# First attention: the products of probabilities and values issued at the end of a step

## The chip, the cores and the metric

The program runs on one core of one Trainium2 chip. The metric is the device time of one execution in microseconds; the median of several runs is compared. Five engines run their own instruction lists and meet through semaphores: TensorE (PE, matrix products and, through them, transposes), VectorE (DVE), ScalarE (ACT), GpSimd (POOL) and SyncE (SP, which only issues DMAs here).

## The reference, cut to what matters

The program computes two layers, each an attention and a mixture of experts, on a residual stream x of 8 batches, 256 tokens and 128 features:

```
x = x + L0_attn(layernorm(x)); x = x + L0_ffn(layernorm(x))
x = x + L1_attn(layernorm(x)); x = x + L1_ffn(layernorm(x))
```

The change lies in the first attention, L0_attn. It has 16 query heads and 4 key heads of 8 features, rotary positions and a causal softmax:

```
q = rope((x @ Wqa @ Wqb).reshape(b, s, 16, 8)); k, v likewise from Wkva, Wkvb, repeated for 4 query heads each
scores = einsum('bqhd,bkhd->bhqk', q, k) * scale          # causal mask, softmax over k -> w
out = einsum('bhqk,bkhd->bqhd', w, v).reshape(b, s, 128) @ Wout + bout
```

L0_ffn follows: a gate chooses two of 8 experts for each token, and the tokens are sorted by expert into 39 tiles. In the kernel this routing is done beside the attention, group by group of batches, and the expert phase begins when the first groups are placed.

## The kernel before, in words

The first attention is a software pipeline over the 8 batches. A **step** is a pair (c, s): c runs from -2 to 10, s over 0, 1, 2, 3, and u = 4c + s numbers it. Each engine has the same loop over the steps (`for c, s in STEPS0`) in its own block, with its own work in each. Within a step TensorE works on several batches at once, in an order that is written out by hand. In the kernel before it is this:

- scores: for batch c, the score products from which the row maxima come (`max_scores`, L1934, three banks), and interleaved with them, for the batch-and-group number p = u - 5, the scores that go to the softmax (`prob_scores0`, L1944 and L1946, three banks). p counts 4 groups for each of 8 batches;
- masks: `masks0` (L1919, L1921) adds the causal mask to the three banks of maxima, so that VectorE may reduce them (`maxima`, L917);
- at s = 0, `turn_max` (L1955) for batch c - 1;
- weighing: `weigh0(u - 6)` (L1970, L1973), 16 products of values and probabilities of group p = u - 6, into bank BO;
- at s = 0, `give_out0(c - 3)` (L2035), the output projection;
- at s = 1, `spread0(c + 1)` (L1982 to L1988), which spreads the rotated queries and keys over the array's rows, in three banks, and `turn_x0(c + 2)` (L1996), the transposes of the normalised input, in one bank;
- at s = 2, `turn_o(c - 2)` (L2018) and `project0(c + 2)` (L2004, L2005, L2009; three banks);
- at s = 3, `turn_back(c - 2)` (L2027);
- where a routing step is due, `route_rows`: `turn_rows` (L1855), `gate_rows` (L1869) or the ranks (`older_rows` and `rank_rows`, L1878 to L1895). For the groups of batches from number 2 on, `gate_rows` is instead issued directly behind the masks.

**The ring of banks.** PSUM has eight banks. Bank BO belongs to the weighing alone; all other products take the next of the seven others in the order of `ring0()` (NRING = 7), and `take` makes TensorE wait until the product that had the bank seven places earlier has been read. `weigh0` takes no bank of the ring. In step (c, 1) the order is three banks of maxima, three of probabilities, three of `spread0`, one of `turn_x0`; in step (c, 2) three, three, one for `turn_o`, three of `project0`.

**What waits for the weighing.** ScalarE's copy of its result, `copy_o0` (L1574): the second half of batch c - 2 in the steps with s = 1, the first half of batch c - 1 in those with s = 3. In a step with s = 1 ScalarE's list is: the exponentials of that step (`exps0`, L1568), `key_copy` (L1548), `copy_o0`, `stack0` (L1554, two copies of the second and third bank of `spread0`). `exps0(p)` waits for the weighing of p - 2. GpSimd masks the probabilities (`mask_probs`, L683) behind the exponentials, and the weighing of p waits for that.

VectorE's list in a step begins with routing (`take_logits`, `choose`, `give_slots`) where it is due, then, by s: `turn` (L898) at s = 3; `residual0` (L951) and `moments_of` at s = 1; `maxima` in every step; `add_max` (L934) and `norm` at s = 0; `normalise` (L941, L944) and `norm_rows` (L1001) later. GpSimd has `mask_probs`, the roots (L668), the sum and difference of the rotation (L692, L698) and the scattering of the rows to the experts' buffer (L738). Behind the last step VectorE stages the first experts' weights (L1117), and TensorE turns the first gathered tile (L2081) once batch 7 has its residual.

Of the kernel before, what the change touches and what calls it, by code (L numbers as in the profile page):

```python
# [18 lines left out]
B, S, D = 8, 256, 128  # L19
# [141 lines left out]
def build(nc, inp, out, last_stage=3):  # L161
    ctx = ExitStack()
    with ctx:
# [204 lines left out]
        def wait(eng, name, b, k):  # L368

            sm, c, before = tables[-1][name]  # L370
            value = b * c + k
            if isinstance(value, int) and value <= 0:
                return
            eng.wait_ge(sm, value + before + 1)

        def signal(ins, name):
            ins.then_inc(tables[-1][name][0], 1)
# [24 lines left out]
        def inside(b):  # L402
            return 0 <= b < B
# [7 lines left out]
        def due(l, u, work):  # L411

            for u0, q in FROM[l].items():
                if u - u0 == AFTER[l][q][work]:
                    return q
            return -1
# [21 lines left out]
        def gates_first(l, q):  # L438
            return q >= COUNTED
# [125 lines left out]
        def _(sp):  # L565
            sp.dma_start(X[:, 0:FIRST, :], inp["x"][0:FIRST].rearrange("t p d -> p t d")).then_inc(x_loaded[0], 16)
            sp.dma_start(misc[:], inp["c_misc"][:, :]).then_inc(ident_loaded, 16)
            for sm in [a for a, _, _ in s0.values()]:
                sp.sem_inc(sm, 1)
# [1250 lines left out]
        def _(pe):  # L1820
# [9 lines left out]
            def take(kind, b, k=0):  # L1830

                assert next(taken) == (kind, b, k)
                at = AT0[kind, b, k] - NRING
                if at >= 0:
                    if RING0[at][0] in ROUTING:
                        for sm, value in routing_read(0, *RING0[at]):
                            pe.wait_ge(sm, value)
                    else:
                        wait(pe, *read_of(*RING0[at]))
                return bank0(kind, b, k)  # L1840
# [6 lines left out]
            def turn_rows(l, q, take):  # L1847

                m = ms[l]
                t0, t1 = TILES[q]  # L1850
                pe.wait_ge(m["normed"], t1 + 1)
                for n in range(rT_banks(q)):
                    bank = take("rT", q, n)
                    for t in range(t0 + 4 * n, min(t0 + 4 * n + 4, t1)):
                        mm = pe.transpose(bank[:, (t - t0 - 4 * n) * P:(t - t0 - 4 * n + 1) * P], rsc[:, t % SLOTS, 0, 0:D], ident)  # L1855
                    mm.then_inc(m["rT"], 1)

            def gate_rows(l, q, take):

                m = ms[l]  # L1860
                if q == 0:
                    pe.wait_ge(w_loaded[l], 16 * (6 if l == 0 else 4))
                pe.wait_ge(m["rT_copied"], sum(rT_banks(a) for a in range(q + 1)) + 1)
                w = D + E if l == 0 else E
                per = 2 if l == 0 else size(q)
                for n in range(gate_banks(l, q)):
                    bank = take("gate", q, n)
                    for t in range(per):
                        mm = pe.matmul(bank[:, t * w:(t + 1) * w], rowsT[:, (per * n + t) * P:(per * n + t + 1) * P], gates[l][:], start=True, stop=True)  # L1869
                    mm.then_inc(m["gated"], 1)  # L1870

            def older_rows(l, q, bank, count):

                t0, t1 = TILES[q]
                h = t1 - t0
                if (l, q) == (0, 0):
                    pe.wait_ge(moe_cast, 3)
                pe.matmul(bank[:, 0:h * E], identb[:], regionb[:].unsqueeze(1).broadcast_to((P, h, E)), start=True, stop=False)  # L1878
                for t in range(t0):
                    pe.matmul(bank[:, 0:h * E], onesb[:], picked[:, t, :].unsqueeze(1).broadcast_to((P, h, E)), start=False, stop=False)  # L1880
                    if count is not None:
                        pe.matmul(count[:, 0:E], onesb[:], picked[:, t, :], start=(t == 0), stop=False)

            def rank_rows(l, q, bank, count):

                m = ms[l]
                t0, t1 = TILES[q]
                h = t1 - t0
                pe.wait_ge(m["picked"], q + 1 + 1)
                for t in range(t0, t1 - 1):  # L1890
                    pe.matmul(bank[:, (t + 1 - t0) * E:h * E], onesb[:], picked[:, t, :].unsqueeze(1).broadcast_to((P, t1 - 1 - t, E)), start=False, stop=False)
                pe.matmul(bank[:, 0:h * E], beforeb[:], picked[:, t0:t1, :].rearrange("p t e -> p (t e)"), start=False, stop=True).then_inc(m["ranked"], 1)
                if count is not None:
                    for t in range(t0, t1):
                        mm = pe.matmul(count[:, 0:E], onesb[:], picked[:, t, :], start=False, stop=(t == t1 - 1))  # L1895
                    mm.then_inc(m["counted"], 1)

            def route_rows(l, u, take):

                q = due(l, u, "turn")  # L1900
                if q >= 0:
                    turn_rows(l, q, take)
                q = due(l, u, "gate")
                if q >= 0 and not gates_first(l, q):
                    gate_rows(l, q, take)
                q = due(l, u, "rank")
                if q >= 0:
                    bank = take("rank", q)
                    count = take("count", q) if q == COUNTED else None
                    older_rows(l, q, bank, count)  # L1910
                    rank_rows(l, q, bank, count)
# [46 lines left out]
            def weigh0(p):  # L1958

                b, g = p // 4, p % 4  # L1960
                half, own = g // 2, g % 2
                wait(pe, "masked", 0, p + 1)
                if g == 0:
                    wait(pe, "v_copied", b, 1)
                    wait(pe, "o_copied", b, 0)
                if g == 2:
                    wait(pe, "o_copied", b, 1)
                values = [vst0[b % 4][:, 4 * t + 2 * half:4 * t + 2 * half + 2, :].rearrange("p a c -> p (a c)")[:, 32 * own:32 * own + 32] for t in range(2)]
                for j in range(4):
                    pe.matmul(ps[32 * j:32 * j + 32, BO, half * S:(half + 1) * S], values[0], probs[p % 2][:, j * S:(j + 1) * S],  # L1970
                              start=(own == 0), stop=False)
                for j in range(4):
                    mm = pe.matmul(ps[32 * j:32 * j + 32, BO, half * S + P:(half + 1) * S], values[1], probs[p % 2][:, 4 * S + j * P:4 * S + (j + 1) * P],  # L1973
                                   start=False, stop=(own == 1))
                signal(mm, "pv")
# [62 lines left out]
            for c, s in STEPS0:  # L2038
                u = 4 * c + s
                if (c, s) == (-2, 2):  # L2040
                    pe.wait_ge(w_copied, 2)
                if (c, s) == (-1, 1):
                    pe.wait_ge(consts_cast, 6)
                    pe.wait_ge(loaded, 16 * 2)
                for part in range(4):
                    if inside(c):
                        max_scores(c, s, part)
                    if 0 <= u - 5 < 4 * B and part < 3:
                        prob_scores0(u - 5, part)
                if inside(c):  # L2050
                    masks0(c, s)
                if due(0, u, "gate") >= COUNTED:
                    gate_rows(0, due(0, u, "gate"), take)
                if s == 0 and inside(c - 1):
                    turn_max(c - 1)
                if 0 <= u - 6 < 4 * B:
                    weigh0(u - 6)
                if s == 0 and inside(c - 3):
                    give_out0(c - 3)
                if (c, s) == (-1, 1):  # L2060
                    turn_x0(1)
                if s == 1 and inside(c + 1):
                    spread0(c + 1)
                if s == 1 and inside(c + 2) and c != -1:
                    turn_x0(c + 2)
                if s == 2 and inside(c - 2):
                    turn_o(c - 2)
                if s == 2 and inside(c + 2):
                    project0(c + 2)
                if s == 3 and inside(c - 2):  # L2070
                    turn_back(c - 2)
                route_rows(0, u, take)
            assert next(taken, None) is None
            wait(pe, "residual", B - 1, 1)
            pe.wait_ge(ms[0]["shared"], sum(gate_banks(0, q) for q in range(LATE)) + 1)
# [265 lines left out]
```

## Time and profile before

| | us |
|---|---|
| median of 3 runs | 568.91 (568.16 to 569.52) |
| span of the profiled execution | 568.9 |
| TensorE busy in it | 482.2 (85%) |
| VectorE busy | 359.5 (63%) |
| ScalarE busy | 296.2 (52%) |
| GpSimd busy | 290.9 (51%) |
| granted TensorE clock, mean | 0.904 of full speed |

The span of the profiled execution and the median of the runs differ by less than 0.1 us. In the rows below, times are microseconds from the start of the span. A row of a timeline gives the start, the duration, the engine, the line of the kernel, the operation, its output and input, their shapes and how many instructions are merged; in brackets stands how long the engine was idle just before, and what ended that. Matrix products are pipelined: the recorded end of one lies behind the start of the next, so that distances are read from start to start. The steps with weighing run from about 47 us (u = 6, which is c = 1, s = 2) to 187 us (u = 37). The spread of step (c, 1) starts at 62.07 for c = 2, at 79.17 for c = 3, at 96.25 for c = 4, at 115.42 for c = 5 and at 135.01 for c = 6; for c = 7 there is none.

### The profile page before, as it was taken

What the parts mean: (1) busy time and instruction counts of PE and PEld (TensorE: products, weight loads), DVE (VectorE), ACT (ScalarE), POOL (GpSimd) and SP (SyncE); (2) the same over time, 40 slices, a digit from 0 to 9 for tenths busy, and PEclk for the clock granted to TensorE, in tenths of its full rate; (3) what the DMA queues carried; (4) which work ended last, traced back from release to release, by engine and by line L of the source; (5) the groups of instructions that cost most, each with busy time, mean ns of one, the idle gap of its engine ahead of it and who ended that gap; (6) DMA issues with size and microseconds to landing.
All of it is one profiled execution on the core that took longest, in us unless ns stands there. A gap on an engine that the chain in (4) does not pass through costs nothing. (4 is left out here: it accounts for less than half of the span.)

```text
span 568.9 us, 14158 instructions
## 1 busy us (share of the span) xinstructions
PE 482.2 (85%) x4435; PEld 384.5 (68%) x4435; DVE 359.5 (63%) x1190; ACT 296.2 (52%) x832; POOL 290.9 (51%) x381
## 2 busy tenths in 40 slices
PE   5779999999998499999667889999899747999980
PEld 3556666656555399999636667677677527899980
DVE  3685677877863535463597788897785863533323
ACT  2224555445553176667536687666753515567650
POOL 3624445448476454565642445443763874356550
PEclk9987999989975589999978899999898977999995
DMA  6999200000000131232199900300000013123217
GB/s 215 323 312 364 88 1 2 1 1 30 13 24 30 43 83 40 81 88 71 34 356 318 318 25 1 150 2 3 20 21 11 30 40 77 55 70 98 72 39 226
DMA packets 28375, 53.71 MB, mean 94 GB/s; under 512 B 4816, under 2 KB 24208, under 8 KB 27248
## 3 DMA queue, kind: packets, MB, share of 16 engines
q1 hardware_dynamic: 23216, 42.17, 23.5%
q0 software_dynamic: 4544, 9.45, 5.0%
q10 hardware_dynamic: 544, 1.20, 0.6%
q8 instruction: 38, 0.62, 0.5%
q14 instruction: 33, 0.27, 0.1%
HBM read 42.32 MB, written 29.81 MB: 127 GB/s over the span
## 5 line engine op out<-in xcount | busy, mean ns | idle before, releaser
L1654 ACT ACTIVATE probs<-ps,w1s 128x128 f32<-128x128 f32 x312 | 89.3, 370 | 47.1 <-PE ps L2090 47.1
L797 POOL DMA_INDIRECT ybuf<-yt,xg x78 | 76.2, 978 | 59.1 <-DVE yt L1183 50.8
L2090 PE MATMUL ps<-xgT,w1s 128*128 128x128 f32 x624 | 86.5, 283 | 1.6 <-ACT xgT L1645 0.9
L738 POOL DMA_INDIRECT xbuf<-rsc,sloti x64 | 63.1, 986 | 40.6 <-DVE sloti L1054 14.8
L2098 PE MATMUL ps<-w,probs 128*128 x624 | 82.2, 276 | 0.0
L2090 PEld LDWEIGHTS ps<-xgT,w1s 128*128 128x128 f32 x624 | 79.1, 199 | 3.4 <-ACT xgT L1645 1.8
L917 DVE TENSOR_REDUCE negm<-ps 128x2 f32<-128x512 f32 (+1 forms) x96 | 60.3, 685 | 27.9 <-PE ps L1921 21.3
L2098 PEld LDWEIGHTS ps<-w,probs 128*128 128x128 f32 x624 | 75.6, 192 | 0.0
L1568 ACT ACTIVATE probs<-ps 128x512 f32<-128x512 f32 x96 | 51.2, 603 | 35.6 <-PE ps L1944 35.1
L1117 DVE COPY w1s<-w 128x516 f32 x78 | 33.9, 434 | 44.0 <-issue 40.2
L683 POOL TENSOR_SCALAR_AFFINE_SELECT probs<-probs 128x512 f32<-128x512 f32 x64 | 39.2, 637 | 40.6 <-ACT probs L1568 40.0
L832 POOL TENSOR_SCALAR_AFFINE_SELECT probs<-probs 128x512 f32<-128x512 f32 x64 | 39.4, 642 | 37.7 <-ACT probs L1757 37.5
L1183 DVE TENSOR_TENSOR yt<-ps,bias 128x128 f32<-128x128 f32 x78 | 22.7, 291 | 46.1 <-PE ps L2098 44.9
L1757 ACT ACTIVATE probs<-ps 128x512 f32<-128x512 f32 x64 | 34.8, 601 | 11.9 <-PE ps L2150 11.9
L1437 DVE SCALAR_TENSOR_TENSOR X<-ps,GT,X 128x128 f32<-128x128 f32 x80 | 27.9, 349 | 7.1 <-PE ps L2190 5.1
L1645 ACT ACTIVATE xgT<-ps 128x128 f32<-128x128 f32 x78 | 22.8, 293 | 18.3 <-PE ps L2081 18.2
L2081 PE MATMUL ps<-misc,xg 128*128 128x128 f32 x78 | 22.2, 287 | 11.4 <-DMA xg<-xbuf 6.9
L2174 PE MATMUL ps<-probs,vst 128*32 128x128 f32 x512 | 22.7, 284 | 8.9 <-POOL probs L832 6.7
L1970 PE MATMUL ps<-probs,vst 128*32 128x256 f32 x256 | 23.5, 444 | 3.4 <-POOL probs L683 3.4
L668 POOL TENSOR_TENSOR rstd<-var,halves 128x4 f32<-128x4 f32 (+2 forms) x17 | 16.9, 996 | 18.4 <-issue 15.3
L1944 PE MATMUL ps<-qst,keys 32*128 32x512 f32 x48 | 21.5, 504 | 5.1 <-DVE qst L934 2.5
L692 POOL TENSOR_TENSOR rot<-rot 128x512 f32<-128x512 f32 x8 | 10.2, 1279 | 28.3 <-DVE rot L898 28.3
(276 smaller groups left out, 1057.6 us busy)
## 6 DMA issues: line engine op xcount, KB each, us to landing
xbuf<-in_c_pads SPq DMA_DIRECT2D x16, 1122.0 KB, 18.8
xg<-xbuf SPq DMA_DIRECT2D x78, 66.0 KB, 1.9
w<-in_w SPq DMA_DIRECT2D x2, 2064.0 KB, 24.0
w<-in_w SPq DMA_DIRECT2D x2, 2048.0 KB, 35.9
w<-ybuf SPq DMA_DIRECT2D x5, 512.0 KB, 5.9
ybuf<-yt,xg POOLq DMA_INDIRECT x78, 2.3
probs<-in_c_sel ACTq DMA_DIRECT2D x2, 512.0 KB, 5.2
bias<-in_b SPq DMA_DIRECT2D x2, 512.0 KB, 31.1
```

What stands on the lines that cost most here:

```text
L683: last = pool.affine_select(out=diag, in_=diag, compare_op=ALU.is_ge, fill=0.0, base=0, pattern=[[0, 4], [1, P]], channel_multiplier=-1)
L738: pool.indirect_dma_start(out=xbuf[l][:, :], out_offset=bass.IndirectOffsetOnAxis(ap=sloti[:, k, t:t + 1], axis=0), in_=rsc[:, t % SLOTS, ...
L797: pool.indirect_dma_start(out=ybuf[l][:, :], out_offset=bass.IndirectOffsetOnAxis(ap=xg[n % AHEAD][:, D:D + 1].bitcast(I32), axis=0), in_= ...
L832: signal(pool.affine_select(out=chunk, in_=chunk, compare_op=ALU.is_ge, fill=0.0, base=0, pattern=[[0, 4], [1, P]], channel_multiplier=-1) ...
L917: signal(dve.tensor_reduce(dst, src, AX.X, ALU.max, negate=True), "maxed")
L1117: dve.tensor_copy(w1s[n % STAGED][:], w1[:, ds(of_tile[n] * W1, W1)]).then_inc(ms[l]["staged"], 1)
L1437: signal(dve.scalar_tensor_tensor(tile, bank1("look", b, look)[:, n * D:(n + 1) * D], GT[:, 2 * b + t, NC - 1 - at - n:NC - at - n], tile, ...
L1568: signal(act.activation(probs[p % 2][:, 512 * n:512 * (n + 1)], bank0("prob", p // 4, 3 * (p % 4) + n), ACT.Exp, scale=QK_SCALE), "probs_d ...
L1654: ins = act.activation(hidT[n % 3][:, c * P:(c + 1) * P], ps[:, q, c * P:(c + 1) * P], ACT.Gelu if l == 0 else ACT.Relu, bias=w[:, FF + c: ...
L1757: signal(act.activation(probs[u % 2][:, n * 4 * P:(n + 1) * 4 * P], bank1("prob", u // 4, 2 * (u % 4) + n), ACT.Copy), "probs_done")
L2090: mm = pe.matmul(ps[:, n % 2, c * P:(c + 1) * P], w[:, c * P:(c + 1) * P], xgT[n % 2][:], start=True, stop=True)
L2098: mm = pe.matmul(ps[:, 6 + n % 2, 0:D], hidT[n % 3][:, c * P:(c + 1) * P], w2[:, ds(e * FF + c * D, D)], start=(c == 0), stop=(c == FC - 1))
```

## The change

`weigh0(u - 6)` is taken from its place behind the masks and `turn_max` and put at the end of the step, behind `route_rows`. Nothing else is changed: the same instructions with the same waits, the same ring of banks, the same lists of the other engines.

```diff
                 if s == 0 and inside(c - 1):
                     turn_max(c - 1)
-                if 0 <= u - 6 < 4 * B:
-                    weigh0(u - 6)
                 if s == 0 and inside(c - 3):
                     give_out0(c - 3)
...
                 if s == 3 and inside(c - 2):
                     turn_back(c - 2)
                 route_rows(0, u, take)
+                if 0 <= u - 6 < 4 * B:
+                    weigh0(u - 6)
```

## Rows read from the trace of the kernel before

**Rows 1.** Windows: busy time by engine, granted clock, DMA share, GB/s, 48 to 190 us and 54 to 104 us

```profile
48.00:190.00 142.00, 131.87 (x1200) 85.26 (x1192) 96.84 (x258) 68.78 (x147) 81.04 (x118) 0.88 0.12 47
54.00:104.00 50.00, 47.84 (x464) 32.27 (x459) 37.91 (x83) 25.89 (x57) 24.76 (x36) 1.00 0.13 51
```

**Rows 2.** Waits of TensorE, 40 to 190 us: total, times, longest

```profile
PE ps L1970 <- POOL probs L683: 3.4, 1, 3.4
```

**Rows 3.** Timeline of TensorE, steps (3, 1), (3, 2) and into (3, 3)

```profile
78.38 0.64 PE L1970 MATMUL ps<-probs,vst 128*32 128x256 f32 x8
...
79.17 0.39 PE L1982 MATMUL ps<-hi,selr 128*128 128x256 f32 x1
...
80.46 0.38 PE L1996 MATMUL ps<-misc,xn 128*128 128x128 f32 x2
80.77 0.39 PE L1934 MATMUL ps<-keys,qst 32*128 32x256 f32 x3
...
81.58 0.46 PE L1946 MATMUL ps<-qst_late,keys 32*128 32x512 f32 x1
81.97 0.50 PE L1921 MATMUL ps<-aboveb,identb 128*128 128x256 bf16 x3
...
83.19 0.66 PE L2018 MATMUL ps<-misc,o 128*128 128x128 f32 x4
83.68 0.60 PE L2004 MATMUL ps<-xnT,wq 128*128 128x256 f32 x2
```

**Rows 4.** Timeline of VectorE and ScalarE, the same steps

```profile
78.34 1.89 DVE L917 TENSOR_REDUCE negm<-ps 128x4 f32<-128x512 f32 x3 [0.20 <-PE ps L1921]
...
80.08 0.38 ACT L1574 ACTIVATE o<-ps 128x256 f32<-128x256 f32 x1
...
80.35 1.09 ACT L1554 ACTIVATE qst<-ps 128x512 fp32r<-128x512 f32 x2
...
82.36 1.89 DVE L917 TENSOR_REDUCE negm<-ps 128x2 f32<-128x512 f32 x3 [2.13 <-PE ps L1921]
```

**Rows 5.** Timeline, step (3, 3): ScalarE's copy behind the weighing

```profile
88.22 0.44 PE L2027 MATMUL ps<-misc,on 128*128 128x128 f32 x2
...
88.35 0.38 ACT L1574 ACTIVATE o<-ps 128x256 f32<-128x256 f32 x1 [0.26 <-PE ps L1973]
```

**Rows 6.** Timeline of VectorE and TensorE, steps (4, 1) and (4, 2)

```profile
95.75 1.89 DVE L917 TENSOR_REDUCE negm<-ps 128x4 f32<-128x512 f32 x3
...
98.12 0.39 PE L1934 MATMUL ps<-keys,qst 32*128 32x256 f32 x3
...
99.05 0.22 PEld L1921 LDWEIGHTS ps<-aboveb,identb 128*128 128x128 bf16 x3 [0.24 <-issue]
```

**Rows 7.** Timeline, step (5, 3)

```profile
122.35 0.22 DVE L1047 TENSOR_TENSOR ranks<-first,ps 128x64 f32<-128x64 f32 x1 [1.12 <-PE ps L1892]
...
123.83 0.46 PE L1944 MATMUL ps<-qst,keys 32*128 32x512 f32 x1 [1.20 <-DVE rot L898]
...
125.82 1.08 PE L1970 MATMUL ps<-probs,vst 128*32 128x256 f32 x8
```

**Rows 8.** Timeline, end of step (6, 3) and step (7, 1)

```profile
142.90 0.63 PE L1855 MATMUL ps<-misc,rsc 128*128 128x128 f32 x4 [0.49 <-DVE negm L917]
...
149.47 0.42 DVE L951 TENSOR_TENSOR X<-X,ps 128x256 f32<-128x256 f32 x1
```

**Rows 9.** Timeline, steps (8, 3) to (9, 1)

```profile
175.74 1.08 PE L1970 MATMUL ps<-probs,vst 128*32 128x256 f32 x8
...
177.26 0.19 DVE L1038 TENSOR_TENSOR picked<-first 128x32 bf16<-128x32 f32 x1
...
177.66 0.23 PE L1878 MATMUL ps<-regionb,identb 128*128 128x32 bf16 x1
...
178.46 0.22 DVE L1047 TENSOR_TENSOR ranks<-first,ps 128x64 f32<-128x64 f32 x1 [1.01 <-PE ps L1892]
...
186.06 1.08 PE L1970 MATMUL ps<-probs,vst 128*32 128x256 f32 x8 [3.39 <-POOL probs L683]
```

## The prediction, written before the changed kernel was run

> **What bounds the kernel now.** First the windows: in the 142 us that hold the weighing TensorE is busy for 131.87, and no other engine reaches 97 [rows 1]. So the stage goes at TensorE's pace, and what counts is each stretch in which it stands still. Next its waits: the only wait of a weighing for its masks is one of 3.4 us [rows 2]. That one, at 186.06, is at u = 37, where the order of the step has nothing to move [rows 9]. So no weighing in its present place waits for anything that a later place could hide. Then the timeline, which shows what the weighing itself hides. It takes 0.79 us from start to start (78.38 to 79.17) [rows 3], and it takes no bank of the ring. While it runs, VectorE reduces the three banks of maxima that the masks have just closed (1.89 us in all) [rows 4]. The next products of the step take just those banks: in (c, 1) the second and third bank of the spread and the bank of `turn_x0` lie seven places behind the three maxima; in (c, 2) the three of `project0` do. That is read from the ring's order, not from a row.
>
> **The change part by part.** Nothing is added or removed: 32 weighings of 16 products keep their waits, and no DMA moves with them. GpSimd's and SP's lists are untouched. I reckon each batch from the start of its masks in (c, 2) against where they start now. A hand-over from one engine to the next I take as 0.14 us: TensorE's third probability product starts at 81.58, ScalarE's second `stack0` ends at 80.35 + 1.09 = 81.44 [rows 3, 4].
>
> *Term A, the spread held back.* In (3, 1) the masks end at 78.38 [rows 3]; VectorE's three reductions end at 78.34 + 1.89 = 80.23, 0.63 apart [rows 4]. `turn_x0` now starts at 80.46, with nothing to wait for. Moved up by the weighing's 0.79 it would start at 79.67, but its bank is free at 80.23 + 0.14 = 80.37. With its own 0.31 (80.46 to 80.77) and then the weighing's 0.79 the step ends at 81.47, against 80.77: 0.70 lost. Of the 0.79 only 0.09 finds work to do. For c = 2 and c = 5 I take the same. For c = 4 VectorE starts its reductions only at 95.75 and ends at 97.64 [rows 6]: 97.64 + 0.14 + 0.31 + 0.79 = 98.88 against 98.12, 0.76 lost. For c = 6 there is no `turn_x0`, and the last bank waits for the second reduction: about 0.41.
>
> *Term B, the copies behind the weighing.* In (c, 1) ScalarE's `copy_o0` waits for this step's weighing, and `stack0`'s two copies stand behind it in ScalarE's list. The second and third probability product of (c, 2) take the banks that these two copies read. Now the weighing is over at 79.17, long before `copy_o0` starts at 80.08. Afterwards it ends last of all, at 81.47. `copy_o0` starts 0.13 later (88.22 to 88.35 [rows 5]), `stack0` 0.27 after that (80.08 to 80.35) and ends 1.09 later: 82.96 [rows 4]. The third product starts at 83.10, the masks 0.39 later (81.58 to 81.97 [rows 3]) at 83.49. They now start at 81.97, so that A and B make 1.52, and B alone 0.82. For c = 2 and 5 I take 1.50. For c = 4: 98.88 + 2.02 = 100.90 against 99.05, 1.85 [rows 6]. For c = 6 the third product waits for the first of the two copies only: A and B about 1.00. B's bounds: 0, if ScalarE's copies overlap the products as now, and 1.1.
>
> *Term C, the projection.* With the weighing gone from between masks and `turn_o`, `project0` starts 0.43 + 0.49 = 0.92 after the masks' start (83.19 less 0.79 and 81.97; 83.19 to 83.68) [rows 3]. Its first bank is that of the first maxima: VectorE starts 0.39 after the masks (81.97 to 82.36), takes 0.63, and 0.14 to hand over: 1.16. So 0.24 for c = 2 and 3 each [rows 3, 4]. For c = 4, 5 and 6 the next step waits for VectorE's later work in any case, and C costs nothing.
>
> *Term D, (5, 3).* Ranks of the routing are due in (5, 2). VectorE is idle for 1.12 us until they come, then turns the rotation, and TensorE waits 1.20 us for that [rows 7]. The ranks now come ahead of the weighing, so VectorE starts 0.6 sooner against the masks, and the weighing covers part of the turn: I take a gain of 0.77. Its bounds are 0 and 1.20 plus what the clock adds. It stood at half, 1.2 GHz, behind that wait: the weighing at 125.82 shows 1.08 us for its first part where 0.64 is usual [rows 7, 3].
>
> *Term E, `turn_rows`* in (4, 3) and (6, 3). It takes the bank of the step's first maxima. At 142.90 it has waited 0.49 us for VectorE [rows 8], with the weighing already done. Afterwards the weighing comes behind that wait, not before it, and only part of its 0.79 falls where the next scores wait anyway. I take a loss of 0.39 and 0.48 (bounds 0 and 0.79 each).
>
> *Term F, (7, 1).* `gate_rows` comes 0.79 sooner, and so does `residual0` (149.47) [rows 8], whose bank the second probability product waits for: a gain of 0.35 (0 to 0.45).
>
> *Term G, the tail.* In (8, 3) the chosen experts are known at 177.26 + 0.19 = 177.45, but TensorE comes to the rank products at 177.66, because weighing and `turn_back` stand ahead, and VectorE goes on at 178.46 [rows 9]. The weighing out of the way, `turn_back` and the older ranks are done by 176.8, the rank products follow the choice at once, and VectorE goes on at about 177.85. The slots, eight scatters, and the last masks, for which the weighing at 186.06 waits, hang on this: a gain of 0.60 (0 to 0.8).
>
> In the steps (c, 0) `turn_max` stands ahead of the weighing before and after, `give_out0` (c from 3 on) moves up, and the next scores wait for `add_max` as now: nothing. In (1, 2), (1, 3) and (2, 0) the readers are early or the order is the same: nothing.
>
> *Sum.* c = 2: 1.50 + 0.24 = 1.74. c = 3: 1.52 + 0.24 = 1.76. c = 4: 1.85 + 0.39 = 2.24. c = 5: 1.50 - 0.77 = 0.73. c = 6: 1.00 + 0.48 = 1.48. c = 7: -0.35. Tail: -0.60. Together 7.0 us later. All behind the stage follows from its end, and keeps its length. The profiled span is 568.9, the median of the runs 568.91, so no correction is due: 568.9 + 7.0 = 575.9 us.
>
> The page "TensorE: Matmul & The Clock Gate" of the Trainium skill (its head table) calls ScalarE's queue strictly first in, first out. By that rule term B stands; if copies could pass one another, `stack0` would not wait for `copy_o0`, and the sum would be lower by B. No row of the kernel before shows a blocked ScalarE copy with ready ones behind it.
>
> **The rivals.**
>
> *Half of it.* Only the ring's wait for VectorE bites (A, C, E), and ScalarE's copies are hidden, say because they are handed over faster. For: `stack0`'s 1.09 us stand beside scores and masks of 1.6 us (80.77 to 82.40). Against: `copy_o0` cannot start before the weighing ends. Without B (0.8 for c = 2, 3 and 5, 1.1 for c = 4, 0.6 for c = 6: 4.1) 2.9 is left: 571.8 us.
>
> *The clock falls.* The new waits split TensorE's work in the steps (c, 1) and (c, 2) of five batches, some 1.7 us in each. Behind the 1.20 us wait of (5, 3) the granted clock was at half [rows 7]; part of a weighing there took 0.44 us more. A spell over a weighing and its neighbours I put at 1.0 to 1.6 us. Three or four spells and A to G: 580 to 582 us. Against it: from 54 to 104 us TensorE stood still for 2.2 us in all, and the clock stayed full [rows 1]. The same page, under "A second HAM failure mode: psum-queue depth-cycling", says that small idle gaps between groups of products, as they arise in cycling through PSUM banks, can make the clock swing between its levels; that would be this case.
>
> *Faster.* VectorE and ScalarE have the banks free in time, because TensorE's slack reaches back to them: the point is whether `turn_x0` can start within 0.1 us of the spread's last product. Then A, B, C and E are zero, D, F and G remain (1.7), and with the clock full in (5, 3) about 1.0 more: 568.9 - 2.7 = 566.2 us. Against: TensorE's products are in order, and the reductions cannot start before the masks.
>
> *Nothing.* TensorE's waits fall where it would have waited later: about 569. Against: the waits of (5, 3) and (4, 3) alone could take up such slack, and I have counted them.
>
> **How the numbers follow.** Forecast, 574 to 578: 0.55. Half of it, 571 to 574: 0.17. The clock, above 578: 0.18. No change: 0.03. Faster: 0.07. The likeliest is 575.9. The range 571.3 to 579.5 leaves out the faster cases and half of the clock's. A difference below 0.2% (1.1 us) is what the measurement can't tell from none. Faster by more 0.06, within it 0.04, slower by more 0.90.
>
> **What would show it.** In (3, 1) and its like the second bank of the spread starts about 0.35 us behind the first, with VectorE's reduction as its releaser, and `turn_x0` 0.14 behind the third reduction (A). ScalarE shows an idle stretch ahead of L1574 that ends with L1973, and TensorE one ahead of L1944 or L1946 that ends with L1554 (B). From (3, 2) to (4, 2) the masks stand 19.2 us apart (17.08 now, from 81.97 to 99.05, with 0.24 of C at c = 3 and 1.85 of A and B at c = 4). The 1.20 us wait of (5, 3) is gone or halved (D), and VectorE's ranks in (8, 3) come 0.4 us behind the choice (G). Wrong would be: no wait for L917 in the spread; a TensorE that stands at 1.2 GHz in stretches from 60 to 120 us; or a stage as long as before with a later stage changed.

## The result

The changed kernel took 578.8 us (median of 4 runs, 575.5 to 580.0). The recorded ratio to the kernel before is 1.0136 with a 95% interval of 1.0088 to 1.0184, which is 7.7 us (5.0 to 10.5) of 568.9; the plain medians, 578.8 and 568.91, lie 9.9 us apart, and a fourth execution of the kernel before, of 1082 us, is left out. In a second set, on another occasion, the changed kernel's median was 582.4 us (6 runs) and the ratio 1.0133 (1.0070 to 1.0197). So it is slower, clear of the noise, by less than 2%. The forecast was 575.9 us, slower. The profiled execution is 578.1 us long, 9.2 more than that of before. All ratios here leave out executions more than 1.5% above the fastest of their kernel.

The page of the changed kernel (busy time by engine, then the tenths of 40 slices):

```profile
span 578.1 us, 14158 instructions
PE 484.6 (84%) x4435; PEld 387.7 (67%) x4435; DVE 359.2 (62%) x1190; ACT 294.3 (51%) x832; POOL 290.3 (50%) x381
PE   4779889889898579999758889999899856999980
PEclk9787897998999579999969899996998976999995
```

The number of instructions is that of before and the busy times are nearly the same, so the 9.2 us are idle time and clock. TensorE's waits from 40 to 200 us (total, times, longest):

```profile
PE ps L1970 <- POOL probs L683: 4.3, 1, 4.3
PE ps L1944 <- ACT qst L1554: 1.9, 3, 0.6
PE ps L1987 <- DVE negm L917: 1.6, 4, 0.4
PE ps L1855 <- DVE negm L917: 1.5, 2, 0.9
PE ps L2004 <- DVE negm L917: 1.2, 4, 0.3
...
PE ps L1944 <- ACT qst_late L1554: 0.6, 1, 0.6
...
PE ps L1944 <- DVE rot L898: 0.4, 1, 0.4
PE ps L1946 <- ACT qst L1554: 0.4, 1, 0.4
```

The same list for the kernel before (40 to 190 us) has no wait for L1554 and none at L1987 or L2004, and it has these two:

```profile
PE ps L1944 <- DVE rot L898: 1.6, 2, 1.2
...
PE ps L1855 <- DVE negm L917: 0.5, 1, 0.5
```

So the waits for L1554 (the copies of term B; five of them, the last in (6, 2)) and those at L1987 (the spread, A) and L2004 (the projection, C; four each) are new. The wait at L1855 (E) has grown, and the one for L898 (D) is down. Steps (3, 1) and (3, 2), TensorE:

```profile
79.75 0.38 PE L1921 MATMUL ps<-aboveb,identb 128*128 128x256 bf16 x2
79.88 0.36 PE L1982 MATMUL ps<-hi,selr 128*128 128x256 f32 x1
...
80.76 0.39 PE L1987 MATMUL ps<-hi,selr 128*128 128x256 f32 x1 [0.40 <-DVE negm L917]
...
82.05 0.41 PE L1996 MATMUL ps<-misc,xn 128*128 128x128 f32 x2
82.39 0.64 PE L1970 MATMUL ps<-probs,vst 128*32 128x256 f32 x8
...
83.18 0.39 PE L1934 MATMUL ps<-keys,qst 32*128 32x256 f32 x3
...
84.33 0.46 PE L1944 MATMUL ps<-qst_late,keys 32*128 32x512 f32 x1 [0.65 <-ACT qst L1554]
...
85.22 0.50 PE L1921 MATMUL ps<-aboveb,identb 128*128 128x256 bf16 x3
85.56 0.60 PE L2018 MATMUL ps<-misc,o 128*128 128x128 f32 x4
86.45 0.75 PE L2004 MATMUL ps<-xnT,wq 128*128 128x256 f32 x2 [0.29 <-DVE negm L917]
```

and VectorE and ScalarE in them:

```profile
80.01 1.89 DVE L917 TENSOR_REDUCE negm<-ps 128x4 f32<-128x512 f32 x3 [0.20 <-PE ps L1921]
...
83.31 0.38 ACT L1574 ACTIVATE o<-ps 128x256 f32<-128x256 f32 x1 [2.34 <-PE ps L1973]
83.59 1.08 ACT L1554 ACTIVATE qst<-ps 128x512 fp32r<-128x512 f32 x2
```

They answer to [rows 3, 4]. The spread's second bank waits 0.40 us for the first reduction; `turn_x0` starts at 82.05, 0.15 behind the third (80.01 + 1.89 = 81.90). ScalarE stands idle for 2.34 us ahead of `copy_o0`, which starts 0.13 behind the weighing (83.18), and TensorE then waits 0.65 us for the first `stack0`. From the masks at 79.75 to those at 85.22 are 5.47 us; before, from the row below to 81.97 [rows 3], 3.90. That is 1.57 for A and B, where 1.52 was reckoned.

```profile
78.07 0.38 PE L1921 MATMUL ps<-aboveb,identb 128*128 128x256 bf16 x2
```

Some of the rest is the clock. In the windows the last number but two is the granted clock, as a share of full speed:

```profile
59.00:64.00 5.00, 5.00 (x39) 3.56 (x34) 2.02 (x4) 2.05 (x4) 1.92 (x3) 0.66 0.26 94
64.00:86.00 22.00, 19.64 (x186) 12.98 (x178) 13.10 (x27) 11.76 (x27) 8.75 (x14) 1.00 0.01 2
86.00:91.00 5.00, 4.71 (x30) 3.65 (x28) 3.51 (x7) 0.65 (x2) 1.56 (x3) 0.66 0.00 0
96.00:101.00 5.00, 4.97 (x40) 3.69 (x39) 4.80 (x15) 0.87 (x3) 2.05 (x3) 0.66 0.02 5
134.00:139.00 5.00, 4.98 (x41) 2.71 (x41) 2.63 (x6) 3.14 (x7) 3.95 (x5) 0.66 0.00 0
...
176.00:188.00 12.00, 9.62 (x106) 6.04 (x105) 5.68 (x26) 7.57 (x18) 10.40 (x17) 1.00 0.07 25
```

A mean of 0.66 over 5 us means that part of the window stood at half clock, 1.2 GHz. Between 59 and 101 us there are three such windows, where the execution of before had full clock from 54 to 104 us [rows 1]; in return the clock is full from 176 to 188 us, in the steps of c = 8, where before it stood at half (0.50). At the start of the experts (L2081) the two executions are 7.1 us apart (205.94 against 198.84); the other 2.1 us arise later, with unchanged code. How much of this belongs to the change and how much to the execution, one profile cannot tell.

### The profile page after: what moved, and what is told of

It reads as the page before. It is cut to its first block and busy times, and to the rows that moved or that the text cites. A ratio compares the mean times of both kernels' runs of the same rounds, so it can differ in the third digit from the quotient of the medians.

```text
span 578.1 us, 14158 instructions
## 1 busy us (share of the span) xinstructions
PE 484.6 (84%) x4435; PEld 387.7 (67%) x4435; DVE 359.2 (62%) x1190; ACT 294.3 (51%) x832; POOL 290.3 (50%) x381
## 5 line engine op out<-in xcount | busy, mean ns | idle before, releaser
L2081 PE MATMUL ps<-misc,xg 128*128 128x128 f32 x78 | 22.1, 287 | 11.8 <-DMA xg<-xbuf 6.9
L1970 PE MATMUL ps<-probs,vst 128*32 128x256 f32 x256 | 22.2, 422 | 4.3 <-POOL probs L683 4.3
L2150 PEld LDWEIGHTS ps<-qst,kst 32*128 32x128 f32 x256 | 17.5, 193 | 11.0 <-issue 9.7
L1944 PE MATMUL ps<-qst,keys 32*128 32x512 f32 x48 | 19.9, 459 | 5.6 <-DVE qst L934 2.5
```

## The experiments

Single executions of one kernel differ by more than the terms in dispute. The kernel before ran 80 times beside the experiments, in 567.1 to 583.3 us, and the executions with a lower mean granted clock were the longer ones. So beside the measured ratio I give the difference at an equal clock: a least-squares fit over the 203 executions whose clock is on record, with one level for each kernel and one slope, which came out as -4.15 us for 0.01 of mean granted clock. Its remaining scatter is 1.7 us for one execution. The last column is the same fit over the 163 executions that the ratios use, with a slope of -3.12 us. Both columns have 95% intervals, and both are only as good as the assumption that one slope serves all kernels and sets.

| kernel | runs | median us | ratio (95%) | at equal clock, us from before | same, executions of the ratio |
|---|---|---|---|---|---|
| changed, both sets | 10 | 579.9 | 1.0136; 1.0133 | +8.1 ± 1.2 | +8.8 ± 1.0 |
| late except at s = 1 | 12 | 576.3 | 1.0062 (1.0017 to 1.0106) | +0.9 ± 1.1 | +2.2 ± 1.0 |
| late only at s = 1 | 12 | 576.5 | 1.0085 (1.0042 to 1.0129) | +8.6 ± 1.1 | +8.4 ± 0.9 |
| changed, `stack0` first | 6 | 579.4 | none | +1.9 ± 1.5 | +3.2 ± 1.9 (2 runs) |
| before, `stack0` first | 12 | 576.3 | 1.0078 (1.0042 to 1.0115) | +1.5 ± 1.1 | +2.8 ± 1.0 |
| changed with filler | 6 | 579.1 | 1.0106 (1.0054 to 1.0157) | +8.4 ± 1.5 | +8.4 ± 1.3 |
| before with filler | 6 | 582.1 | 1.0147 (1.0079 to 1.0215) | +6.7 ± 1.5 | +7.5 ± 1.3 |
| late only at routing, both sets | 23 | 567.7 | 0.9937 (0.9904 to 0.9971); 0.9945 (0.9906 to 0.9984) | -2.0 ± 0.8 | -1.9 ± 0.7 |
| late only in (5, 2) | 12 | 571.8 | 1.0034 (0.9995 to 1.0073) | +0.5 ± 1.1 | +0.9 ± 0.9 |
| late only in (8, 3) | 12 | 572.1 | 1.0033 (1.0002 to 1.0065) | -1.8 ± 1.1 | -1.0 ± 0.9 |
| at routing, `stack0` first | 12 | 570.2 | 1.0013 (0.9982 to 1.0043) | -3.0 ± 1.1 | -1.9 ± 0.9 |

The sharper instrument is the distance between the masks of one step (c, 0) and the next in a stretch of full clock. From (3, 0) to (4, 0) it is 17.08 to 17.10 us in five traces with the old order there. Only from (6, 0) to (7, 0) is it less steady, as told below.

**Where the loss sits.** Two runs, each the other's counterpart: the diff is that of the first, and the second has the two conditions exchanged.

```diff
-                if 0 <= u - 6 < 4 * B:                       # behind the masks
+                if 0 <= u - 6 < 4 * B and s == 1:
...
+                if 0 <= u - 6 < 4 * B and s != 1:            # behind route_rows
```

> The weighing goes to the end of the step in all steps except those with s = 1, where it stays directly behind the masks. Theory (terms A and B sit in the steps with s = 1): C, E, D, F and G are left, 0.48 + 0.87 - 0.77 - 0.35 - 0.60 = -0.4 us, so 568.5 us, same as before to within 0.2%. TensorE's wait for L1554 and the one of L1987 for L917 are gone. Rival 'it is the late place in general' (spread evenly over the 32 weighings): three quarters of the loss stay, 574 to 576. Rival 'the clock': no certain number, but half-clock stretches between 60 and 120 us remain.

> Only in the steps with s = 1 is the weighing put behind the spread and the transposes of the input; all others stay directly behind the masks. Theory: A and B in full for c = 2 to 6, 1.5 + 1.5 + 1.85 + 1.5 + 1.0 = 7.4 us, so 576.3 us (575 to 578.5 with half-clock stretches as in the changed kernel); nearly the whole loss with five moved weighings that count. Rival 'the late place in general': a quarter of the loss, 571. Without term B: 3.3 us, 572.2.

Late everywhere but at s = 1: 0.9 us at an equal clock (2.2 in the last column), most of the loss gone; by the ratio, 3.5 us (1.0 to 6.0) remain, in executions whose clock was on average lower (0.888 against 0.895). The expected -0.4 is missed: C and E cost more and D and F give less than reckoned, as shown below, and with their measured sizes 0.1 to 1.3 us more than before are left (an estimate, with and without G and with the two values of E in (6, 3)). The waits for L1554 and those at L1987 are gone. Late only at s = 1: +8.6 us at an equal clock, not told apart from the whole; its ratio is 4.9 us (2.4 to 7.4), with a mean clock of 0.907. The masks (3, 0) to (4, 0) stand 18.66 us apart (72.24 to 90.90, clock full) against 17.08: 1.58. So the loss is in the steps with s = 1. A loss spread over all 32 weighings would be 2 us here, and is out.

**The two halves, A and B.** In ScalarE's list `stack0` goes ahead of `copy_o0`.

```diff
+                if s == 1 and inside(c + 1):
+                    stack0(c + 1)
                 if s == 1 and inside(c - 2):
                     copy_o0(c - 2, 1)
-                if s == 1 and inside(c + 1):
-                    stack0(c + 1)
```

> The changed kernel, but in ScalarE's list stack0 stands ahead of copy_o0 in the steps with s = 1. Theory: B goes (4.1 us), A, C, E, D, F, G stay: 571.8 us, and about 4 us under the changed kernel. TensorE's 0.65 us waits for L1554 at L1944 in (2, 2), (3, 2), (4, 2), (5, 2) are gone, those for L917 at L1987 stay. Rival 'all of it is VectorE's reductions': no change against the changed kernel, 576 to 579. Rival 'the clock': with the largest waits gone the half-clock stretches between 60 and 120 us go too, and the gain is over 5 us.

> Control for the run before it: the kernel before with the same exchange in ScalarE's list, weighings in their old place. Theory: nothing waits for the order there, except that the third probability product of the steps (c, 2) already starts 0.14 us behind the second stack0: up to 0.27 us sooner in each of four steps, 568 to 569 us. Rival 'the exchange is good by itself': 565 to 567.

In the changed kernel this brought 6.2 us at an equal clock (8.1 to 1.9; 5.6 in the last column, on two executions). TensorE's waits from 60 to 140 us:

```profile
PE ps L1987 <- DVE negm L917: 1.9, 4, 0.7
PE ps L2004 <- DVE negm L917: 1.2, 4, 0.3
PE ps L1934 <- DVE negm L917: 0.8, 3, 0.3
PE ps L1855 <- DVE negm L917: 0.5, 1, 0.5
PE ps L1944 <- DVE rot L898: 0.4, 1, 0.4
```

Those for L1554 are gone, those of A and C stay, as expected. The distance (3, 0) to (4, 0) falls from 19.04 to 17.90 us, and 0.82 over the 17.08 of before remain. The control has 16.94 there, 0.14 less than before, as expected. The halves can be read from the masks of (c, 1) to those of (c, 2), all at full clock:

| c | before | before, `stack0` first | changed, `stack0` first | changed |
|---|---|---|---|---|
| 2 | 3.90 | 3.74 | 4.33 | 5.46 |
| 3 | 3.90 | 3.74 | 4.33 | 5.47 |
| 4 | 3.91 | 3.87 | 4.67 | 5.80 |
| 5 | 3.91 | 3.74 | 4.32 | 5.47 |
| 6 | 3.42 | 3.38 | 3.96 | 4.63 |

(The changed kernel's from its second profile; before at c = 5 and 6 from its own profile; 3.38 from the kernel late at routing with `stack0` first, as the control stood at half clock there.) Between the two columns with `stack0` first nothing but the weighing's place differs: that is A, 3.1 us in the five batches, reckoned 3.3. The exchange gives 5.2 us in the changed kernel and 0.6 in the kernel before: 4.7 for B, reckoned 4.1. Yet the control's total was slower than before, by the ratio (4.4 us) and at an equal clock (1.5). At full clock, from 53 to 101 us, no step of its trace is longer than before; where the rest comes from stays open.

**Is TensorE really standing still there?** Products that nothing reads are added where it waits.

```diff
                 bank = take("prob", b, 3 * g + n)
+                if n == 0 and (p + 5) % 4 == 2 and 2 <= (p + 5) // 4 <= 6:
+                    for _ in range(3): ...      # zerob by aboveb, 512 columns, into bank
...
                 bank = take("sel", b, 0)
+                if b >= 3: ...                  # the same, one of 512 and one of 256 columns
```

> The changed kernel once more, beside the others of this call: in the call before, single executions of the kernel before lay between 568.5 and 582.3 us, lower times with a higher mean granted clock, so a comparison needs both on one chip and enough executions. Theory (A to G sum to 7.0 at an equal clock): 7 us over the kernel before at an equal mean clock, and 18.8 us from the masks of one step (c, 0) to those of the next where the clock is full between them, against 17.1. Rival 'the clock alone': no difference at an equal mean clock.

> The changed kernel with products added whose results nothing reads, in the steps of c = 2 to 6: two (512 and 256 columns, bf16) ahead of the spread in the bank that it takes, three of 512 columns ahead of the first probability product of (c, 2) in its bank; about 1.0 us of TensorE work for each batch at full clock, 5 us in all. Theory: TensorE stands still there for VectorE (A) and for ScalarE (B), so the work is free: masks (c, 0) to (c + 1, 0) stay 18.8 us apart at full clock, the time that of the changed kernel to within 1 us at an equal clock. Rival 'TensorE has no slack there; the new order costs because of the array or the issue of its instructions': 5 us more. Rival 'the gaps lower the clock': the filler raises the mean granted clock and the time falls below the changed kernel's.

> Control: the same added products in the kernel before. Theory: nothing hides them but the few tenths for the third probability product, 0.8 to 1.0 us for each batch of c = 2 to 6: 18.0 us from masks to masks at full clock in place of 17.1, and 4 to 5 us more than before. Rival: free here too, 0 to 1 us.

The added work is free in the changed kernel (8.4 against 8.1 us at an equal clock) and costs 6.7 us in the kernel before, where 4 to 5 were reckoned. Masks (3, 0) and (4, 0), first in the changed kernel's second profile, then with filler, then before with filler:

```profile
72.23 0.82 PE L1919 MATMUL ps<-aboveb,identb 128*128 128x512 bf16 x3
91.27 0.82 PE L1919 MATMUL ps<-aboveb,identb 128*128 128x512 bf16 x3
```
```profile
75.45 0.82 PE L1919 MATMUL ps<-aboveb,identb 128*128 128x512 bf16 x3
94.50 0.82 PE L1919 MATMUL ps<-aboveb,identb 128*128 128x512 bf16 x3
```
```profile
73.07 0.82 PE L1919 MATMUL ps<-aboveb,identb 128*128 128x512 bf16 x3
91.16 0.82 PE L1919 MATMUL ps<-aboveb,identb 128*128 128x512 bf16 x3
```

These are 19.04, 19.05 and 18.09 us, against 17.08 before. One microsecond of products vanishes in the waits of A and B, and costs 1.01 us where there are none. At c = 6, where these waits are shorter, it is not all hidden: 17.62 us from (6, 0) to (7, 0) against 17.21. In the trace with filler the waits for L1554 are gone, covered. The filler did not raise the clock: the mean over its executions was 0.899, against 0.898 of the changed kernel. So the rival with the clock gets no support either.

**The gains alone.** The weighing stays behind the masks, except where gates or ranks are due.

```diff
+                late = due(0, u, "gate") >= 0 or due(0, u, "rank") >= 0
+                if 0 <= u - 6 < 4 * B and not late: weigh0(u - 6)     # behind the masks
...
+                if 0 <= u - 6 < 4 * B and late: weigh0(u - 6)         # behind route_rows
```

(`late` written out in both places; in the parts it is `u == 22` and `u == 35`; the last has ScalarE's exchange besides.)

> The weighing goes behind the routing only in steps where gates or ranks are due (u = 20, 22, 28, 30, 35, 39), and stays behind the masks in all others. Theory: D, F and G without A, B and E: 0.77 + 0.35 + 0.60 = 1.7 us under the kernel before at an equal clock, 567.2 us on a base of 568.9. Rival 'nothing of D, F, G reaches the end': the same as before. Rival 'C in (5, 2) outweighs D': up to 0.5 us slower.

> The kernel with the weighing behind the routing only where gates or ranks are due, once more, on another chip time and beside its parts. The call before measured 0.9937 of the kernel before, 3.6 us, and 2.4 us at an equal clock. Theory (D, F, G): 1.7 us under before at an equal clock. Rival 'a lucky share of full clock': no difference here, ratio 0.998 to 1.002.

> Only the weighing of u = 22, step (5, 2), goes behind projection and ranks. Theory D: VectorE's wait for the ranks falls from 1.1 to about 0.7 us, TensorE's wait of 1.2 us for L898 to about 0.4, and masks (5, 0) to (6, 0) stand 19.4 us apart at full clock (21.55 less the 20.96 of the changed kernel gives 0.6 for it, so before about 20.0). In the total 0.6 to 0.8 us less, not told apart from zero by the timing alone. Rival: the wait stays and the distance is 20.0.

> Only the weighing of u = 35, step (8, 3), goes behind the ranks. Theory G: VectorE's ranks come 0.36 us behind the start-to-end of the choice in place of 1.01, and from the gates of (8, 3) at half clock to the start of the experts 0.6 us less than the 25.2 us of before (173.62 to 198.84). In the total 0.6 us less. Rival: GpSimd is the bound there, and nothing changes.

> The kernel with the weighing late only at gates and ranks, and ScalarE's stack0 ahead of copy_o0. Theory: D, F and G, and 0.15 us for each of (2, 2) to (5, 2), where the exchange brought the masks (c, 0) to (c + 1, 0) from 17.08 to 16.94: 0.6 us under the kernel without the exchange at an equal clock. Rival from the timing of the exchange alone (1.7 us slower than before at an equal clock): 1 to 2 us over it.

The kernel late only at routing is faster than the kernel before, and so than the changed one, in two sets: 3.6 and 3.1 us by the ratios, 2.0 at an equal clock (1.7 reckoned). Of its parts neither is faster by the ratio, and one, late only in (8, 3), is slower by it (1.0002 to 1.0065) and faster at an equal clock. The timing of a single part is too coarse for terms of 0.6 us; the traces carry them. The step (5, 3) in the kernel late only at routing, behind late ranks, and in the kernel late only in (8, 3), where (5, 2) is as before:

```profile
121.40 0.46 PE L1944 MATMUL ps<-qst,keys 32*128 32x512 f32 x1 [0.42 <-DVE rot L898]
```
```profile
121.97 0.47 PE L1944 MATMUL ps<-qst,keys 32*128 32x512 f32 x1 [1.21 <-DVE rot L898]
```

The masks (5, 0) to (6, 0) stand 19.41 us apart in the first (106.52 to 125.93), 19.96 in the second (106.53 to 126.49). Of the 0.55 only 0.41 lie behind the late ranks, from the masks of (5, 2) to those of (5, 3): 6.42 against 6.83 us. The kernel late only in (5, 2) has 6.43 there and a wait of 0.42 for L898, so D is 0.4 us; its whole distance of 19.4 could not be read, because the clock was at half behind (5, 0). The other 0.16 lie in (5, 0) to (5, 1), 5.55 against 5.71, where gates are due and the weighing now stands behind them.

In (8, 3), with the weighing late at routing, VectorE's ranks come

```profile
173.48 0.19 DVE L1038 TENSOR_TENSOR picked<-first 128x32 bf16<-128x32 f32 x1
174.06 0.22 DVE L1047 TENSOR_TENSOR ranks<-first,ps 128x64 f32<-128x64 f32 x1 [0.38 <-PE ps L1892]
```

0.39 us behind the choice at half clock, against 1.01 [rows 9]; and from the gates (169.84) to the experts (194.42) are 24.58 us, against 25.22 (173.62 to 198.84), the clock at 0.50 in both: 0.64, the whole of G. The kernel late at routing with `stack0` first, also at 0.50, has 24.58 again. In the kernel late only in (5, 2) the gates and ranks of (8, 3) ran at full clock, and the ranks came 0.36 us behind the choice with the weighing in its old place. So the ranks' part of G shows at half clock alone. The kernel late only in (8, 3), built to try G, ran them at full clock too (0.36), so it says nothing on G at half clock. ScalarE's exchange on top gave 1.0 us at an equal clock (nothing in the last column) and lost 3.9 by the ratios of one set (1.0013 against 0.9945): not told apart.

## Why the prediction was right

The direction and the mechanism held: the ring of banks and the order of ScalarE's copies, not GpSimd's masks, set what the weighing's place is worth. In distances at full clock, the masks (c, 0) to (c + 1, 0):

| from | before | changed | difference | reckoned |
|---|---|---|---|---|
| (2, 0) | 17.09 | 19.03 | 1.94 | 1.74 |
| (3, 0) | 17.08 | 19.04 | 1.96 | 1.76 |
| (4, 0) | 18.10 | 20.60 | 2.50 | 2.24 |
| (5, 0) | 19.96 | 20.96 | 1.00 | 0.73 |
| (6, 0) | 15.91 | 17.21 | 1.30 | 1.48 |
| (7, 0) to (7, 1) | 5.70 | 5.55 | -0.15 | -0.35 |

(The changed kernel's from its second profile, (4, 0) from that with filler, where the second profile stood at half clock; before from its profile, (5, 0) from the kernel late only in (8, 3).) The sum is 8.55 us, 7.9 with G; reckoned 7.6 and 7.0; at an equal clock 8.1 ± 1.2 were measured.

- **The time itself** was helped by luck. The forecast starts from 568.9, the median of three executions; over 80 later ones the median of the kernel before is 571.6, and that of the changed kernel's ten is 579.9, above the range of 571.3 to 579.5. The first set fell inside it with 578.8, the second, with 582.4, did not. What the forecast had right is the difference, not the base.
- **A and B** were right: 7.8 us in the five batches, where 7.4 were reckoned; A is 3.1 of 3.3, B 4.7 of 4.1.
- **C** was mis-sized: from the masks of (3, 2) to those of (3, 3) 5.42 us (82.56 to 87.98 in the second profile) against 5.03, 0.39 where 0.24 stood. The projection starts 1.23 us behind the masks, not 1.16, and its first pair of products takes 0.67 us in place of 0.60.
- **D** was mis-sized: 0.41, not 0.77. The wait for L898 fell from 1.21 to 0.42 as said, and VectorE's for the ranks from 1.12 to 0.72 us, but not all of that reaches the next masks.
- **The steps (c, 0)** were put at nothing, but (5, 0) to (5, 1) became 0.16 us shorter.
- **E** was right in kind, with the wait at L1855 in (6, 3) from 0.49 to 0.94 us in the first profile, and mis-sized. From the masks of (4, 3) to those of (5, 0) are 3.91 us against 3.29, a loss of 0.62 where 0.39 stood. In (6, 3) it depends on VectorE, as told below the list.
- **F** was 0.15 of the 0.35.
- **G** was right at half clock, 0.64; at full clock the ranks have nothing to gain. In the changed kernel's profile the clock was full there, and the ranks came 0.36 us behind the choice.
- **The rivals.** *Half of it* is out: the waits for L1554 are there. *Faster* and *nothing* are out. *The clock* was partly right, and its sign of being wrong came true: the first profile has three new windows with half clock between 59 and 101 us. But the second profile of the changed kernel has none between 48 and 103 us (it stood at half from there to about 107), and the mean clock over all its executions (0.898) is no lower than that of before (0.895). So the new waits show no effect on the mean clock. The swing between levels, which the page "TensorE: Matmul & The Clock Gate" of the Trainium skill describes under "A second HAM failure mode: psum-queue depth-cycling", is there in the profiles of before and changed alike; that the new small gaps made more of it, no run shows.
- On ScalarE's strict order ("TensorE: Matmul & The Clock Gate", head table) the trace agrees: ScalarE is idle for 2.34 us ahead of L1574 (80.97 to 83.31), while the spread's second bank, whose copy stands behind it in the list, is done by 81.5; with the copies exchanged TensorE's waits for them are gone.

**The step (6, 3).** From its masks to those of (7, 0) are 4.30 us in the changed kernel's second profile. With the weighing in its old place it is 3.68 or 3.69 in three traces (late only at s = 1, before with `stack0` first, before with filler), 4.22 in the trace of before and 4.56 in the kernel late only in (8, 3), all at full clock. The four `norm_rows` ahead of VectorE's reductions take 1.37, 1.90 and 2.24 us there from start to end. In the trace of before:

```profile
140.25 1.90 DVE L1001 TENSOR_SCALAR rsc<-X,mv,rstd 128x256 f32<-128x256 f32 x4
```

In the changed kernel they take 1.37. Like for like E costs 0.62 here as in (4, 3); against the profile of before it costs 0.08. The wait of 0.49 us that the term was built on [rows 8] came with the longer `norm_rows`: in the three traces with 1.37 there is none. Why they run longer in some executions, no run shows.

## What to carry to other kernels

Work that takes no bank of a shared ring can be a cover: put it between the products whose banks are still being read and the ones that take them, and count the ring's length before moving it. Ask also which in-order list holds the reader of what you move, and what stands behind that reader. Move such work only past the instructions that another engine is waiting for, as the kernel late only at routing does, and leave the cover elsewhere.

## What the hardware showed that was not expected

The same program took 567.1 to 583.3 us in 80 executions, and the granted clock goes with it: 4.15 us for 0.01 of the mean in the fit over all kernels. In the profiles the half-clock stretches lie at other places from one execution to the next, in the same code: before, from about 163 to 203 us without a break; in the kernel late only in (5, 2), whose order in these steps is the same, from 168 to 172 and again from 181 to 203 us. A wait does not decide it alone. Behind the 1.20 us wait of (5, 3) the clock was at half in the profile of before [rows 7]; in the kernel late only in (8, 3) the same wait, 1.21 us, stood in a stretch at full clock throughout:

```profile
64.00:158.00 94.00, 89.27 (x871) 58.88 (x863) 74.93 (x191) 49.78 (x107) 51.06 (x76) 1.00 0.03 8
```

So a change worth under 1% of this kernel needs a dozen executions of either side or more (an estimate from the 1.7 us of scatter that the clock leaves: about 1.4 us on a difference of twelve and twelve), or a distance read inside a stretch of one clock.
